# A carried state in a linear-attention layer: eight multiply-adds on VectorE for a product on GpSimd and a sum on VectorE

## The reference, cut to what matters

```python
def step(kv, inp):
    qi, ki, vi = inp
    scores = jnp.einsum('bhtd,bhsd->bhts', qi, ki) * mask
    o = jnp.einsum('bhts,bhsd->bhtd', scores, vi) + jnp.einsum('bhtd,bhde->bhte', qi * q_dec, kv)
    kv = blk_dec * kv + jnp.einsum('bhtd,bhte->bhde', ki * k_dec, vi)
    return (kv, o)
```

## Time and profile before

| what | value |
|---|---|
| median of 3 runs | 536.89 us (532.29 to 537.02) |
| profiled execution | 539.22 us, its span 537.5 us |
| granted TensorE clock, mean | 0.939 |
| PE busy | 424.8 us (79%) |
| DVE busy | 351.0 us (65%) |
| ACT busy | 241.2 us (45%) |
| POOL busy | 195.6 us (36%) |
| loop over the chunks of layer 1 | from about 331 to 524 us of the span |

### The profile page before, as it was taken

The page is one execution under the profiler, slowest core; times in us unless marked ns, Lnnn a source line. Parts: engine busy times, 40 slices in busy tenths (PEclk is TensorE's granted clock), DMA queues, the critical chain, the costliest instruction groups (busy, mean ns, idle before and its releaser), DMA issues.

```text
span 537.5 us, 10677 instructions
## 1 busy us (share of the span) xinstructions
PE 424.8 (79%) x4188; PEld 197.1 (37%) x4188; DVE 351.0 (65%) x584; ACT 241.2 (45%) x471; POOL 195.6 (36%) x309
## 2 busy tenths in 40 slices
PE   6797788878788787788686896596888798869766
PEld 3253213232222222221242552344544463446544
DVE  5878768778788878786255285876368627862640
ACT  1575476877776777767566210431111111121220
POOL 3022515252322222130210146638338716780530
PEclk9997789999999999998799597888999998999989
DMA  7632240414202020200000032221022102300000
GB/s 225 225 77 68 78 159 16 169 30 164 64 3 66 2 68 2 67 2 2 2 1 1 1 117 79 79 80 41 1 79 99 40 2 79 119 21 1 22 3 20
DMA packets 19094, 31.92 MB, mean 59 GB/s; under 512 B 2544, under 2 KB 7120, under 8 KB 18724
## 3 DMA queue, kind: packets, MB, share of 16 engines
q1 hardware_dynamic: 19044, 31.23, 18.1%
HBM read 13.20 MB, written 8.06 MB: 40 GB/s over the span
## 4 chain that ended last, share of the span: by engine, by line
PE 35%; issue 18%; POOL 18%; ACT 10%; DVE 8%; DMA 6%; SPq 5%; POOLq 0%; ACTq 0%; DVEq 0%
PE PS L669 9%; ACT prob L1402 7%; PE PS L651 6%; POOL vdec L1562 6%; POOL qr L1554 5%; POOL xn L1571 5%; DVE pmax L1088 4%; DMA k_op<-k_scr 4%; SPq L471 3%; PE PS L583 3%; PE PS L587 2%; PE PS L784 2%; POOL kr L1554 1%; PE PS L540 1%; PE PS L880 1%
## 5 line engine op out<-in xcount | busy, mean ns | idle before, releaser
L1088 DVE TENSOR_REDUCE pmax<-PS 128x8 f32<-128x1024 f32 x144 | 171.9, 1222 | 49.8 <-PE PS L583 33.4
L1402 ACT ACTIVATE prob<-PS 128x512 f32<-128x512 f32 (+1 forms) x320 | 159.9, 552 | 73.5 <-PE PS L651 70.5
L1533 POOL TENSOR_SCALAR_AFFINE_SELECT prob<-prob 128x512 f32<-128x512 f32 x64 | 39.9, 635 | 179.7 <-ACT prob L1402 179.7
L651 PE MATMUL PS<-q_op,k_op 55*128 55x512 bf16 (+3 forms) x384 | 61.7, 342 | 43.8 <-ACT prob L1402 41.1
L669 PE MATMUL PS<-prob,vaug 128*16 128x512 f32 (+3 forms) x768 | 83.7, 526 | 0.0
L583 PE MATMUL PS<-k_op,q_op 52*128 52x128 bf16 (+3 forms) x576 | 58.5, 279 | 9.1 <-DVE pmax L1088 4.6
L651 PEld LDWEIGHTS PS<-q_op,k_op 55*128 55x128 bf16 x384 | 18.4, 94 | 125.4 <-ACT prob L1402 108.7
L1571 POOL TENSOR_TENSOR xn<-state,c_sb 128x512 f32<-128x512 f32 x28 | 29.3, 1046 | 81.5 <-DVE state L1271 56.4
L1426 ACT COPY vk<-PS 128x512 f32<-128x512 f32 x16 | 9.4, 585 | 86.5 <-PE PS L795 86.5
L784 PE MATMUL PS<-xnT,w_sb 128*128 128x512 f32 x80 | 44.0, 650 | 0.6 <-DVE by_sin L1238 0.6
L1554 POOL TENSOR_TENSOR qr<-qr,turned 128x512 f32<-128x512 f32 x32 | 40.0, 1269 | 4.9 <-DMA turned<-by_sin 4.8
(11 more groups left out here) (181 smaller groups left out, 527.2 us busy)
## 6 DMA issues: line engine op xcount, KB each, us to landing
turned<-by_sin SPq DMA_DIRECT2D x80, 128.0 KB, 2.0
k_op<-k_scr SPq DMA_DIRECT2D x14, 220.0 KB
q_op<-q_scr SPq DMA_DIRECT2D x14, 208.0 KB
c_sb<-const_dram SPq DMA_DIRECT2D x1, 2060.0 KB, 7.2
w_sb<-w_dram SPq DMA_DIRECT2D x1, 1876.5 KB, 7.6
q_scr<-part_a SPq DMA_DIRECT2D x6, 256.0 KB, 3.5
k_scr<-part_a SPq DMA_DIRECT2D x6, 256.0 KB, 3.8
q_scr<-part_b SPq DMA_DIRECT2D x6, 256.0 KB, 3.4
```

What stands on the lines that cost most here:

```text
L651: last = mm(PS[:, (GH * s + h) % ST_BANKS, at:at + nn], k_op[rows, slot, h // 2, P * j:P * j + P], q_op[rows, slot, h // 2, P * i0:P * i0 ...
L1088: vec.tensor_reduce(pmax[:, of_pair, at:at + step * (TPS - 1) + 1:step], both.rearrange("p a (b c) -> p a b c", c=P), AX.X, ALU.max).then_ ...
L1402: sca.activation(prob[:, s % P_SLOTS, h, 0:UNIT_W[u]], PS[:, k % ST_BANKS, 0:UNIT_W[u]], ACT.Exp).then_inc(s_exp, 1)
L1533: po.affine_select(out=blk, in_=blk, compare_op=ALU.is_ge, fill=0.0, base=0, pattern=[[0, GH], [1, P]], channel_multiplier=-1).then_inc(s_ ...
```

## The change

VectorE no longer adds `faded` in one instruction. For each of the 8 blocks of 64 columns it issues one SCALAR_TENSOR_TENSOR: the old state's block (SBUF) times the decay of that block (one number a partition, read from SBUF through a pointer), plus the block of new sums (PSUM). Only the last of the eight raises `s_state`. In place of the wait for `faded` there is a wait for VectorE's own last state. GpSimd's `fade_state`, the view `faded` and the semaphore `s_faded` go.

```diff
-        faded = xn[:, 0:QT // 2, :].rearrange("p (k o) (q e) -> p (k o q) e", k=QT // 2, q=2)
...
                 if u % SPB:
-                    v.wait_ge(s_faded, fades(u))
+                    v.wait_ge(s_state, states(u))
                 new = PS[:, (6, 3)[s], :].rearrange("p (k e) -> p k e", e=D1)
                 dst = state[:, (u + 1) % STATES, :, :]
                 if u % SPB == 0:
                     vec.tensor_copy(dst, new).then_inc(s_state, 1)
                 else:
-                    vec.tensor_tensor(dst, new, faded, ALU.add).then_inc(s_state, 1)
+                    for k in range(QT):
+                        last = vec.scalar_tensor_tensor(out=dst[:, k, :], in0=state[:, u % STATES, k, :], scalar=K["blkdec"][:, k:k + 1],
+                                                        in1=new[:, k, :], op0=ALU.mult, op1=ALU.add)
+                    last.then_inc(s_state, 1)
...
-            def fade_state(u):
-                if u % SPB in (0, SPB - 1):
-                    return
-                g_.wait_ge(s_state, states(u))
-                fade = K["blkdec"].rearrange("p (k o) -> p k o", o=1).broadcast_to([P, QT, D1])
-                po.tensor_tensor(faded, state[:, u % STATES, :, :], fade, ALU.mult).then_inc(s_faded, 1)
...
-                fade_state(2 * c + 1)
                 if c + 1 < NCH:
                     fade_v(c + 1)
-                    fade_state(2 * c + 2)
```

More of the change, by code:

```diff
@@ L324, in build @@
         s_kv = sem("s_kv")
-        s_state, s_faded = sem("s_state"), sem("s_faded")
+        s_state = sem("s_state")
         s_o, s_oT = sem("s_o"), sem("s_oT")
@@ L394, in states @@
             return u - u // SPB
-        def fades(u):
-            return u - u // SPB - (u + 1) // SPB
         def half_of(s):
```

## The result

| | before | after |
|---|---|---|
| median | 536.95 us | 559.58 us (556.83 to 562.94, 4 runs) |
| ratio after to before, 95% interval | | 1.045 [1.039, 1.051] |
| profiled execution, its span | 539.22, 537.5 us | 557.49, 555.7 us |
| first state to the end of the span | 197.44 us | 220.09 us |
| last state to the end of the span | 17.94 us | 23.52 us |

The change costs 22.6 us. The profiled executions differ by 18.3, but layer 0, which is the same, was 4.45 us shorter in the one of after (the first state of layer 1 starts at 335.61, before at 340.06). From there to the end the difference is 22.65 us, so I use that stretch, the loop, to compare traces.

A forecast was written before the change was run, and what follows sets the result against it. The latency of a chain through both state advances, no engine full, was taken to bound the loop. Longer stretches +19.1 us, less 2.0 coming back, net +17: 556 us for a profiled execution, 554 for the median, range 545 to 566.

The forecast's parts named there:

- the likeliest case: Whole kernel: the eight start 0.21 us apart, 0.02 either side, clock about as before; 548 to 560 us, chance 0.70.
- Price of an instruction: Each VectorE advance: eight starts 0.21 us apart, last 0.29 long, result after 1.76 us (before 0.69).
- the sum of 19.1: Layer 1's loop: new minus old stretch, first advance to waiting matmuls, over 28 advances in all kinds of chunk, +19.1 us.
- nothing between the advances: Chunks 2, 3, 6, 10, 11, 12, 14: stretch from 2.78 to 3.74 us, +0.96 each, 6.7 in all.
- one rope: Chunks 1 and 4, one rope between the advances: stretch from 2.77 to 4.79 us, +2.02 each, 4.0 in all.
- Rope and store: Chunks 5 and 9, rope and the store's addition between advances: stretch 3.93 to 5.39 us, +1.46 each, 2.9 in all.
- The signs named: Trace checks, among them POOL busy time down 29 us and TensorE's idle time before the scores from 0.78 to about 1.7.
- What comes back: VectorE's two-SBUF-input products, chunk 2's query product and the router's, run faster as GpSimd loses 28 products: 2.0 us back.
- The clock: Rival: longer TensorE gaps bring five more falls of its granted clock, costing 8 us: +25, 562 us; chance 0.09.
- the free pointer: Rival: the eight start 0.145 us apart, the pointer costing nothing: +3, 540 us; chance 0.08.
- The faster case: Rival: the hop through GpSimd outweighs the eight, starting 0.07 us apart: -10, 527 us; chance 0.03.
- No overlap: Rival's extreme: the eight run without overlap, 2.32 us per advance: +33, 570 us; 0.10 shared with 0.257 apart, 565 us.

The follow-up runs named there:

- e1: The changed kernel with the number 0.5 in place of the decay read through a pointer: 1.006 of the kernel before, 542.0 us.
- e3: The kernel before with its one sum of 512 columns split into eight of 64, GpSimd's product kept: 1.051 of the kernel before, 564.1 us.
- e8: The changed kernel with GpSimd's rotations of each span's fourth chunk held until that chunk's first masks are done: 1.028 of the kernel before.
- the split sum: The kernel before with its 512-column sum split into eight, GpSimd's product kept: 1.051; with unread matmuls in TensorE's gaps, 1.015.

## Why the prediction held, point by point

- **Forecast**: 554, range 545 to 566; measured 559.6, in the range and at the upper end of the likeliest case (548 to 560). Slower, as 0.89 had it. The mechanism was right: both advances lie on one chain, and the period grows with the stretch.
- **Price of an instruction**: 0.21 apart and 1.76 to the result were taken; measured 0.19, 0.272 long, 1.61. Scaled down from 512 columns the distance came out at 0.22, 0.03 too long: the pointer adds 0.08 there and 0.06 here, and the rest without it would be 0.14 where 0.13 was measured. Why is open; the estimate by the lengths, 0.205, was nearer. The pointer's 0.06 is shown by e1. With the measured price the sum of 19.1 becomes 15.6: 0.74 x 7, 1.72 x 2, 1.16 x 2, 0.95, 0.92 x 4. (Two asides of the prediction were slightly off: by its own sum 0.19 apart gives +13, not 12, and 0.23 apart +21, not 22. Nothing hangs on them.)
- **The page's rule**: the Trainium skill, "VectorE: DVE Perf Modes", its section on the TRN2 errata, gives an estimate of 0.19 for 64 columns from PSUM. The trace has 0.19 with a pointer, but 0.13 without (e1, e3), so the agreement is by accident; the earlier trace rows already ran 0.06 under it.
- **Kinds of chunk**: nothing between the advances, +0.96 forecast, +0.74 in chunk 12; one rope, +2.02 forecast, 4.49 - 2.77 = +1.72 in the stretch of chunk 4; that nothing is saved there, since GpSimd's product was hidden, held. Rope and store: the stretch as forecast by the corrected price, 5.09.
- **The signs named**: POOL's busy time fell from 195.6 to 168.4 us, 27 for the 29 forecast. TensorE's idle time before the scores did not grow from 0.78 to 1.7 but fell to 0.59 in chunk 12: the carry ahead of it now waits 0.99 for the first state, where it didn't wait before, and the two share the longer stretch.
- **What comes back** is the step that failed. I took 2.0 us back because GpSimd does less. The product for the queries of chunk 2 did return to 1.21, but the router's product met the rotations, 1.27 us each, instead of `vdec`, 0.6 each. Chunk 6 before, to be read beside the rows of e8:

```profile
422.13 2.32 POOL L1562 TENSOR_TENSOR vdec<-vk,c_sb 128x256 f32<-128x256 f32 x4
...
423.34 0.59 DVE L1195 TENSOR_TENSOR apart<-apart 128x32 f32<-128x32 f32 x1
...
425.42 2.48 POOL L1554 TENSOR_TENSOR qr<-qr,turned 128x512 f32<-128x512 f32 x2
```

With `fade_state` gone the rotations start 2.48 us behind the first advance instead of 5.05, and the product comes later, 3.71 instead of 2.97. Its mean went from 592 to 1025 ns. What GpSimd no longer does matters less than what then runs at that moment.

- **The clock** was a rival with 0.09, priced at 1.6 us a fall in the mix of one chunk, and was not taken into the forecast. It came in part: more falls in the loop, and one through the last output that alone cost over 4 us in the profiled execution. The forecast's "most of them pass at full clock" counted the gaps of before; now TensorE waits for the state 24.6 us in 18 gaps instead of 13.4 in 13. That the sum landed as near as it did was luck, two errors of opposite sign: 3.5 too dear on the eight, some 9 too little on clock and GpSimd.
- **Rivals**: the free pointer would have been 540; it is not free, and e1, without a pointer, gave 542 beside 537.8. The faster case needed starts under about 0.12 apart; even without a pointer they are 0.13 apart. No overlap (570) is out, 0.19 against 0.27.

## What to carry to other kernels

On a chain that passes through two engines, an instruction is priced by the distance to the next start and by when its result is there; eight small ones with a pointer scalar, 0.19 us apart, cost more than a wide product on another engine, a hop and a wide sum (3.52 against 2.78 us), although one fused instruction, with one number for all heads, won 1.8%. Look at each place of the chain separately: where the other engine's product is already hidden, taking it over saves nothing and costs all of it. And when a change lengthens TensorE's waits, add the clock to the bill, and test it with unread matmuls in the gaps, of both kernels: what filling gives the changed one alone is not yet the change's share.

## What the runs showed of the hardware

- A pointer scalar adds 0.06 us to each SCALAR_TENSOR_TENSOR even when eight follow each other without a wait (0.19 against 0.13 apart, 272 against 211 ns).
- The cost of a wait of TensorE is not only its length. Behind gaps such as those of 1.53 and 1.57 us above, matmuls ran at about half the clock (1.96 us where 1.09 is full speed), and later those of the last output for most of its 9.56 us, in code that the change doesn't touch. The length of the gap alone doesn't decide it: in the same trace the mixes of chunks 6 and 10, behind gaps of 1.54 and 1.74 us, took 1.09, as at full clock. Filling the gaps with work that is thrown away gave the unchanged kernel 1.6%, the changed one 1.8% and the split sum 3.5%.
- A 32-column product of VectorE with both inputs in SBUF took 1.31 us beside GpSimd's 1.25 us rotations and 0.19 without them; the SCALAR_TENSOR_TENSORs, one tensor input in SBUF and one in PSUM, kept 267 to 283 ns all the time, in chunk 5 beside the rotations too. The Trainium skill, "SBUF — State Buffer", "Who interferes with whom", says that a VectorE instruction with two SBUF inputs contends with a GpSimd instruction that reads SBUF, and that one with at most one, outside the two-port modes, doesn't. The traces agree. They add that the pointer scalar in SBUF didn't count as a second input.
